# Macaron block on one core: weighings of the attention in pairs, earlier projections at its end, and two weight splits in other places

## The chip, the cores and the metric

The kernel runs on one core of a Trainium2 chip. The metric is the device time of one execution in microseconds (us); lower is better. Engine names as in the profile: PE is TensorE's matmul side and PEld its weight loads, DVE is VectorE, ACT is ScalarE, POOL is GpSimd, SP is SyncE, which here only issues transfers.

## What is computed

One macaron block over 2,048 tokens of width 512: half a mixture of experts, causal attention, half a mixture of experts, each behind a layer norm and added to the residual.

```python
x = x + 0.5 * ffn(layernorm(x))      # 8 experts, the best 2 of each token, width 256, SiLU gate
x = x + attention(layernorm(x))      # 16 query heads, 4 key heads of 32, rotary, causal, softmax, @ wo
x = x + 0.5 * ffn(layernorm(x))      # the same experts once more
```

Everything is float32. The expert matmuls are made of high and low parts of the operands (`WH`, `WL`, `XH`, `XL`): `WH` is a rounded copy of the weights `WR`, `WL` is `WR - WH`, and a product is the sum of three matmuls.

## The kernel before

All engines run fixed programs, tied by semaphores; each engine works through its own queue in order. The stages follow each other: router and layer norm (`*_first`), routing 0 (`dve_route`, `pe_route`, `act_route` with f = 0), 39 expert tiles (`*_experts`), projections of the attention (`*_project`), the attention with the next router inside it (`*_attend`), routing 1 and 39 expert tiles again (f = 1).

**The attention's plan.** `attend_plan` writes one list of steps; each engine walks through it and does its own part of each step. The work is cut into 16 groups G (a block b = G // 4 of 512 queries, one key head, its 4 query heads). Group G has 4b + 4 key tiles k of 128 keys; a tile is numbered n. A tile has four `score` steps (one matmul for each head, line L1674), each followed on ACT by an exponential into a buffer `P4` (L1774). A `weigh` step (L1688) multiplies the four heads' exponentials with V in four narrow matmuls of 32 output columns each, which run side by side in the array, into bank 3; where PE also sums the exponentials, a `sum` of the same form follows (L1706, into bank 4), at a group's last tile also one of `CD` (L1697). Before the change, `weigh` of tile n - 1 stands behind the fourth score of tile n. Groups from 8 on have four `P4` buffers, n modulo 4.

**The tops.** Between the scores stand `top` steps for a later group: a matmul of queries by keys (L998) whose maximum DVE takes (L1011, with a mask L1013). Their banks are 5, 6 and 7 in a ring, and for part of groups 8 to 13 bank 4 as well, lent from one group's `even` to the first `sum` of the next. Scores take banks 0 to 2 in turn (after the last top five banks).

**The sums besides PE.** In groups 8 to 14 POOL adds some tiles into `CH` (`link`, four additions of a head each, L1848), and transfers that accumulate add others, and at last `CH`, into `CD` (`onto`, L1864); POOL issues those. The group's last `weigh` step waits for the last of these transfers. On the diagonal POOL also masks the exponentials (L1834).

**The end of the attention.** After group 15, ACT makes `WH` of four experts (L568, `split1`), the last projections `("proj", 3, c)` run (L1723, four matmuls over the groups 12 to 15, index k, for each c), DVE adds the residual (L1902), takes the statistics and a root by Newton (`norm1`, with a square root on ACT, L341), ACT scales (`scale1`, L1791), PE transposes (`turn`, L389), ACT copies the transposed tile (L400) and the kept residual (`keep`, L1798), and `logits` (L414) and `best` end the router. Banks come from `Ring.take` in the plan's order.

**Routing.** `dve_route` computes the expert tiles' slots and tokens (`TK`, on which the gathers wait), with `EI` (the expert of each tile) behind the large masks `LL`, and `slots` a long matmul of PE (L734). `low_in_between` is one `WL` (L574) inside it, used only for f = 1.

Of the kernel before, what the change touches and what calls it, by code (L numbers as in the profile page):

```python
# [9 lines left out]
NE = 8  # L10
# [581 lines left out]
def dve_route(g, f, R, low_in_between=None):  # L592
# [63 lines left out]
    for h in range(2):  # L656
# [10 lines left out]
        for q in range(2 * h, 2 * h + 2):  # L667
# [1 line left out]
                              ps.HF[:, 1, 8 * q:8 * q + 8].unsqueeze(2).to_broadcast([P, 8, P]),  # L669
                              ALU.is_equal).then_inc(rt.sem, 1)  # L670
            out["LL", q] = rt.up()
    if low_in_between:
        low_in_between()
    dve.tensor_tensor(ps.en, r.ba[:], ps.tl, ALU.add).then_inc(rt.sem, 1)
    dve.wait_ge(rt.sem, rt.up())
    dve.tensor_tensor(r.cj[:], K[:, C_IOTAJ:C_IOTAJ + NJ * NE].rearrange("p (j e) -> p j e", e=NE),
# [5 lines left out]
    dve.wait_ge(rt.sem, rt.up())  # L682
    dve.tensor_copy(r.EI[:], ps.EF).then_inc(rt.sem, 1)
    out["EI"] = rt.up()
    dve.wait_ge(s(f"slots{f}"), 1)
    sl = bk(g, 2)
    if f == 0:
# [834 lines left out]
    return LINKS[n + first_two[1] - k] if k == first_two[0] else LINKS[n]  # L1522


def finish_plan(b):

    todo = [[("proj", b, c)] for c in range(4)]
    todo += [[("stats", b, c)] for c in range(4)]
    todo += [[("store", b), ("solve", b)]]
    todo += [[("scale", b, c)] for c in range(4)]  # L1530
    todo += [[("turn", 4 * b + c)] for c in range(4)]
    return todo + [[("logits", b)], [("best", b)]]


def attend_plan(g):
# [15 lines left out]
    for n, (G, k) in enumerate(TILES):  # L1551
        b = G // 4
        for j in range(4):
# [22 lines left out]
            if j == 3 and n:  # L1576
                if known and known[0][0] <= at and free and n - 1 not in LAST.values():
                    solved.append(known.pop(0)[1])
                    plan.append(("solvemax", solved[0]))
                plan.append(("weigh", n - 1))  # L1580
                if n - 1 in LAST.values():
                    G0 = TILES[n - 1][0]
                    plan.append(("out", G0))
                    free = False
                    put(at + 1, ("recip", G0))
                    put(at + 3, ("even", G0))
                    if G0 % 4 == 3:
                        if b == 1:
                            residual(at + 2, 0)
                        until = at + (34 if b == 1 else 9)  # L1590
                        put(until, ("finish", G0 // 4))
                        residual(until + 62, G0 // 4 + 1)
# [6 lines left out]
            assert told > G, (told, G)  # L1599
    assert not later and not extra and not ahead, (later, extra, len(ahead))  # L1600
    plan += [("weigh", len(TILES) - 1), ("out", 15), ("up1", 4), ("split1", 0), ("split1", 1), ("split1", 2), ("split1", 3), ("recip", 15), ("even", 15)]
    for c in range(4):
        plan += [("proj", 3, c), ("norm1", c), ("scale1", c)] + ([("turn", 12 + c - 2), ("keep", c - 2)] if c >= 2 else [])
    plan += [("turn", 14), ("turn", 15), ("keep", 2), ("keep", 3), ("split1", 4), ("split1", 5), ("split1", 6), ("split1", 7)]
    plan += [("logits", 3), ("best", 3), ("store", 3)]
    ring.set_banks([5, 6, 7], ring.n)
    g.lent, g.back = range(7, 13), {}
# [2 lines left out]
    g.wide = min(4 * step[1] + step[2] for step in plan[last + 8:] if step[0] == "score")  # L1610
    for step in plan:
        if step == ("proj", 3, 0):
            ring.set_banks([5, 6, 7, 0, 2, 1], 5)
        if step == ("score", g.wide // 4, g.wide % 4):
            g.wide_after = {bank: ring.uses[bank] for bank in (5, 6)}
            ring.set_banks([7])
# [36 lines left out]
def pe_attend(g):  # L1653
# [56 lines left out]
    def proj(key):  # L1710
        _, b, c = key
        bank = pe_take(g, key)
        if b == 0 and c == 0:
            pe.wait_ge(s("wo"), 16)
        if b == 3:
            pe.wait_ge(s("exp"), 4 * len(TILES))
        if b == 3 and c < 3:
            pe.wait_ge(s("even"), 15)
            pe.wait_ge(s("norm"), c + 1)
        else:  # L1720
            pe.wait_ge(s("even"), 4 * b + 4)
        for k in range(4):
            ins = pe.matmul(bk(g, bank), a.OTs[b % 2][:, k, c * P:c * P + P], a.WO[:, k, :], start=(k == 0), stop=(k == 3))  # L1723
        ins.then_inc(s(f"full{bank}"), 1)

# [330 lines left out]
def build(nc, d, out):  # L2056
    ctx = ExitStack()
    with ctx:
# [20 lines left out]
        act_first(g)  # L2079
        dve_first(g)  # L2080

        g.routed[0] = dve_route(g, 0, g.R0)
        for e in range(5, NE):
            dve_low(g, 0, e)
        for bank in range(8):
            pe.wait_ge(s(f"free{bank}"), 3)
# [31 lines left out]
        g.routed[1] = dve_route(g, 1, g.R1, low1)  # L2118
        pe_route(g, 1)
        act_route(g, 1)  # L2120
        sp_down1(g)

        def residual_stored():
# [67 lines left out]
```

## Time and profile before

| | |
|---|---|
| median of 3 runs | 1263.03 us (1262.26 to 1265.78) |
| the profiled execution's own time | 1267.54 us |
| its span, first to last instruction | 1266.3 us |
| busy: PE, DVE, ACT, POOL | 1174.0, 905.0, 670.7, 601.7 us |
| mean granted clock of PE | 0.986 of full speed |
| groups 8 to 11 (by the first exponential of each) | 599.67 to 781.32 us |
| groups 12 to 14 | 781.32 to 958.97 us |
| last matmul of group 15, first gather of the second experts | 997.5, 1045.20 us |

All durations below are of the one profiled execution; it took 4.5 us more than the runs' median, so differences are worked out inside it and then taken off the median. A matmul's busy time is modelled with its pipeline in it, so that PE seems full even where it issues late: the intervals between starts tell more than the durations.

### The profile page before, as it was taken

What the parts mean: (1) busy time and instruction counts of PE and PEld (TensorE: products, weight loads), DVE (VectorE), ACT (ScalarE), POOL (GpSimd) and SP (SyncE); (2) the same over time, 40 slices, a digit from 0 to 9 for tenths busy, and PEclk for the clock granted to TensorE, in tenths of its full rate; (3) what the DMA queues carried; (4) which work ended last, traced back from release to release, by engine and by line L of the source; (5) the groups of instructions that cost most, each with busy time, mean ns of one, the idle gap of its engine ahead of it and who ended that gap; (6) DMA issues with size and microseconds to landing.
All of it is one profiled execution on the core that took longest, in us unless ns stands there. A gap on an engine that the chain in (4) does not pass through costs nothing.

```text
span 1266.3 us, 20984 instructions
## 1 busy us (share of the span) xinstructions
PE 1174.0 (93%) x6830; PEld 752.6 (59%) x6837; DVE 905.0 (71%) x2116; ACT 670.7 (53%) x1322; POOL 601.7 (48%) x496
## 2 busy tenths in 40 slices
PE   4899999989999999999999999999999878999996
PEld 3578888858786544444445455445443356777774
DVE  7767777769998676576678787678755775666664
ACT  2545555537666554354456566356577744445442
POOL 5844544313210111001527655556592555888886
PEclk9899999999999999999999999999999989999999
DMA  9923333556530032023345845556632453556565
GB/s 340 366 92 109 108 109 109 175 169 127 94 67 4 35 68 35 1 79 75 83 134 135 168 109 128 176 143 163 148 77 61 144 200 74 100 101 100 103 102 74
DMA packets 68552, 148.44 MB, mean 117 GB/s; under 512 B 8832, under 2 KB 29312, under 8 KB 64448
## 3 DMA queue, kind: packets, MB, share of 16 engines
q0 software_dynamic: 35184, 93.34, 34.3%
q1 hardware_dynamic: 33264, 53.77, 12.4%
q8 instruction: 59, 0.97, 0.3%
q14 instruction: 45, 0.37, 0.1%
HBM read 81.28 MB, written 33.55 MB: 91 GB/s over the span
## 4 chain that ended last, share of the span: by engine, by line
PE 55%; DVE 17%; DMA 10%; issue 7%; POOL 7%; ACT 4%; SPq 0%; DVEq 0%; POOLq 0%; ACTq 0%
PE bank L840 9%; PE bank L1674 8%; PE bank L1688 8%; PE bank L998 7%; PE bank L863 5%; PE bank L1723 4%; DVE PM L1011 4%; POOL out L790 4%; DMA out<-Y,DI 4%; PE bank L1706 4%; DVE bank L1013 3%; PE bank L1433 3%; DMA XG<-xn,TK 2%; DMA CD<-P 2%; PE bank L822 2%
## 5 line engine op out<-in xcount | busy, mean ns | idle before, releaser
L1774 ACT ACTIVATE P<-bank 128x512 f32<-128x512 f32 (+3 forms) x640 | 304.4, 534 | 250.2 <-PE bank L1674 241.1
L1011 DVE TENSOR_REDUCE PM<-bank 128x1 f32<-128x512 f32 x384 | 252.3, 683 | 62.0 <-PE bank L998 61.3
L1674 PE MATMUL bank<-Qs,Ks 98*128 98x512 f32 (+3 forms) x640 | 242.2, 408 | 4.6 <-ACT P L1774 3.4
L998 PE MATMUL bank<-Ks,Qs 96*128 96x512 f32 (+3 forms) x640 | 234.5, 387 | 12.2 <-DVE PM L1013 6.1
L1674 PEld LDWEIGHTS bank<-Qs,Ks 98*128 98x128 f32 x640 | 116.6, 189 | 140.5 <-ACT P L1774 74.2
L1834 POOL TENSOR_SCALAR_AFFINE_SELECT P<-P 128x512 f32<-128x512 f32 x64 | 44.2, 702 | 270.6 <-ACT P L1774 229.1
L998 PEld LDWEIGHTS bank<-Ks,Qs 96*128 96x128 f32 x640 | 121.1, 190 | 60.8 <-DVE PM L1011 22.3
L1688 PE MATMUL bank<-P,V 128*32 128x512 f32 (+3 forms) x1280 | 151.7, 546 | 4.3 <-POOL P L1834 4.3
L1013 DVE CUSTOM_DVE_ANT_0 bank<-bank,KB 128x128 f32<-128x128 f32 (+3 forms) x256 | 124.1, 495 | 40.6 <-PE bank L998 39.9
L790 POOL DMA_INDIRECT out<-Y,DI x78 | 129.1, 1655 | 38.7 <-issue 31.8
L1848 POOL TENSOR_TENSOR CH<-CH,P 128x512 f32<-128x512 f32 x108 | 139.4, 1444 | 14.0 <-ACT P L1774 13.4
L952 DVE TENSOR_TENSOR DL<-W,DH 128x512 fp32r<-128x512 f32 x152 | 98.3, 688 | 41.4 <-ACT DH L913 41.4
L767 POOL DMA_INDIRECT XG<-xn,TK x78 | 93.4, 1198 | 32.6 <-issue 16.5
L913 ACT CAST DH<-W 128x512 fp32r x152 | 86.7, 618 | 20.9 <-issue 20.9
L840 PE MATMUL bank<-WH,XH 128*128 x312 | 92.4, 418 | 0.9 <-issue 0.6
L840 PE MATMUL bank<-WL,XH 128*128 x312 | 85.7, 396 | 1.3 <-DVE XL L934 1.3
L840 PE MATMUL bank<-WH,XL 128*128 x312 | 85.5, 395 | 0.0
L779 POOL DMA_INDIRECT y<-Y,DI x39 | 38.7, 993 | 97.1 <-DVE Y L962 97.1
L934 DVE TENSOR_TENSOR XL<-bank,XH 128x512 fp32r<-128x512 f32 x78 | 53.9, 691 | 35.2 <-ACT XH L893 35.2
L899 ACT ACTIVATE G<-bank 128x256 f32<-128x256 f32 x78 | 29.9, 384 | 84.4 <-PE bank L840 84.4
L893 ACT CAST XH<-bank 128x512 fp32r<-128x512 f32 x78 | 45.8, 587 | 47.2 <-PE bank L822 44.1
L1706 PE MATMUL bank<-P,ones 128*32 128x512 f32 (+3 forms) x664 | 69.0, 487 | 1.3 <-DVE PM L1011 1.3
(194 smaller groups left out, 1935.6 us busy)
## 6 DMA issues: line engine op xcount, KB each, us to landing
CD<-P POOLq DMA_DIRECT2D x17, 1024.0 KB, 6.9
xn<-XN SPq DMA_DIRECT2D x8, 1024.0 KB, 9.5
WR<-L_ffn_w POOLq DMA_DIRECT2D x16, 512.0 KB, 15.2
XO<-y POOLq DMA_DIRECT2D x8, 1024.0 KB, 9.5
WR<-L_ffn_w SPq DMA_DIRECT2D x16, 512.0 KB, 7.9
CD<-P SPq DMA_DIRECT2D x7, 1024.0 KB, 4.7
CD<-CH POOLq DMA_DIRECT2D x7, 1024.0 KB, 6.9
XA<-y POOLq DMA_DIRECT2D x24, 256.0 KB, 4.0
```

What stands on the lines that cost most here:

```text
L767: pool.indirect_dma_start(out=x.XG[:, j % NG, :], out_offset=None, in_=g.xnd[f][:, :], in_offset=bass.IndirectOffsetOnAxis(ap=r.TK[:, j:j ...
L790: pool.indirect_dma_start(out=g.out.rearrange("t (h d) -> (t h) d", h=2), out_offset=bass.IndirectOffsetOnAxis(ap=r.DI2[:, h, j:j + 1], ax ...
L840: ins = pe.matmul(bk(g, 2 + j % 2), part[:, k * P:k * P + P], w[:, bass.ds(ev[j] * 2048 + k * 512, 512)], start=(n == 0 and k == 0), stop= ...
L952: ins = dve.tensor_tensor(x.DL[:, k, :], W.W3[:, bass.ds(e * 1024 + k * 512, 512)], DHf[:, k, :], ALU.subtract)
L998: pe.matmul(bk(g, bank)[:, 0:n], g.Qs[b][0:96, G % 4 * 4 + h, c * P:c * P + P], g.Ks[0:96, G % 4, k * BQ:k * BQ + n], start=True, stop=Tru ...
L1011: dve.tensor_reduce(dst, bk(g, bank)[:, 0:n], AX.X, ALU.max).then_inc(s(f"free{bank}"), 1)
L1013: dve.tensor_tensor_reduce(out=bk(g, bank)[:, 0:n], in0=bk(g, bank)[:, 0:n], in1=g.KB[:, CB_MASK + BQ - n:CB_MASK + BQ], scale=1.0, scalar ...
L1674: pe.matmul(bk(g, bank)[:, o:BQ], g.Ks[0:98, G % 4, k * P:k * P + P], g.Qs[G // 4][0:98, G % 4 * 4 + j, o:BQ], start=True, stop=True).then ...
L1688: ins = pe.matmul(bk(g, 3)[32 * h:32 * h + 32, o:BQ], g.V[:, k, q * HD:q * HD + HD], a.P4[buffer_of(n)][:, h, o:BQ], start=(k == 0), stop= ...
L1706: ins = pe.matmul(bk(g, 4)[32 * h:32 * h + 32, o:BQ], g.ones[:], a.P4[buffer_of(n)][:, h, o:BQ], start=fresh, stop=last)
L1774: act.activation(a.P4[buffer_of(n)][:, j, o:BQ], bk(g, score_bank(g, i))[:, o:BQ], ACT.Exp, scale=scale).then_inc(s("exp"), 1)
L1848: ins = pool.tensor_tensor(to[:, h, :], two[:, h, :], one[:, h, :], ALU.add)
```

## The change

Four edits:

1. `weighed_at`: in groups 8 to 14 the weighings of tiles k - 1 and k (k odd) stand one behind the other after the fourth score of the tile after k. In the other groups nothing changes.
2. The last projections: the first three matmuls of each c wait only for groups 12 to 14, the fourth for group 15's part. The ring gets bank 4 as a seventh one. Steps after the third c are reordered: turn 13 and keep 1 before the last tile is scaled.
3. The last `split1` (ACT's `WH` of the eighth expert) moves behind ACT's exponential of routing 1.
4. `low_in_between` moves from before `EI` to after it, and is now used in routing 0 as well: one of the three `WL` that DVE made after routing 0 stands before the wait for `slots`.

```diff
@@ dve_route
-    if low_in_between:
-        low_in_between()
     dve.tensor_tensor(ps.en, r.ba[:], ps.tl, ALU.add).then_inc(rt.sem, 1)
...
     out["EI"] = rt.up()
+    if low_in_between:
+        low_in_between()
     dve.wait_ge(s(f"slots{f}"), 1)
@@
+def weighed_at(n):
+    if not n:
+        return ()
+    G, k = TILES[n - 1]
+    if G < 8 or G == 15:
+        return (n - 1,)
+    return (n - 2, n - 1) if k % 2 else ()
@@ attend_plan
-                plan.append(("weigh", n - 1))
+                plan += [("weigh", m) for m in weighed_at(n)]
...
-    for c in range(4):
-        plan += [("proj", 3, c), ("norm1", c), ("scale1", c)] + ([("turn", 12 + c - 2), ("keep", c - 2)] if c >= 2 else [])
-    plan += [("turn", 14), ("turn", 15), ("keep", 2), ("keep", 3), ("split1", 4), ("split1", 5), ("split1", 6), ("split1", 7)]
+    for c in range(3):
+        plan += [("proj", 3, c), ("norm1", c), ("scale1", c)]
+    plan += [("turn", 12), ("keep", 0), ("proj", 3, 3), ("turn", 13), ("norm1", 3), ("keep", 1), ("turn", 14), ("scale1", 3)]
+    plan += [("turn", 15), ("keep", 2), ("keep", 3), ("split1", 4), ("split1", 5), ("split1", 6)]
...
-            ring.set_banks([5, 6, 7, 0, 2, 1], 5)
+            ring.set_banks([5, 6, 7, 0, 2, 1, 4], 6)
@@ pe_attend, proj
-        if b == 3 and c < 3:
             pe.wait_ge(s("even"), 15)
-            pe.wait_ge(s("norm"), c + 1)
...
         for k in range(4):
+            if b == 3 and k == 3:
+                if c < 3:
+                    pe.wait_ge(s("norm"), c + 1)
+                else:
+                    pe.wait_ge(s("even"), 16)
@@ build
-        g.routed[0] = dve_route(g, 0, g.R0)
-        for e in range(5, NE):
+        g.routed[0] = dve_route(g, 0, g.R0, low0)
+        for e in range(6, NE):
...
         act_route(g, 1)
+        act_high(g, 1, NE - 1)
```

**Place 1: PE at the start of group 10.** The first piece is PE's program before: scores (L1674 or L1685), tops (L998) and a weighing (L1688 or L1699) of one `P4` buffer. Names such as bank1 are pairs of banks.

```order
L998 MATMUL bank3<-Ks_137,Qs2_135 128x512
L1688 MATMUL bank1<-P40_155,V_138 32x512 x4
L1674 MATMUL bank1<-Qs2_135,Ks_137 128x512
L998 MATMUL bank3<-Ks_137,Qs2_135 128x512
L1674 MATMUL bank0<-Qs2_135,Ks_137 128x512
L998 MATMUL bank2<-Ks_137,Qs2_135 128x512
```

The same place in the changed program:

```order
L1685 MATMUL bank1<-Qs2_135,Ks_137 128x512
L998 MATMUL bank2<-Ks_137,Qs2_135 128x128
L998 MATMUL bank3<-Ks_137,Qs2_135 128x512
L1699 MATMUL bank1<-P40_155,V_138 32x512 x4
L1699 MATMUL bank1<-P41_156,V_138 32x512 x4
L1685 MATMUL bank0<-Qs2_135,Ks_137 128x512
```

The weighing of buffer 0 moved four scores back, behind those of the following tile, and stands directly before that of buffer 1; two returns from narrow to wide matmuls became one.

**Place 2: PE at the end of the attention.** Before, with the semaphores that a row waits for (L1723 is the projection, one group of four for each c):

```order
L1723 MATMUL bank<-WO,OT_160 128x512 [waits even,norm,exp,free5]
L1723 MATMUL bank<-WO,OT_160 128x512 x3
L1723 MATMUL bank<-WO,OT_160 128x512 [waits even,norm,exp,free6]
L1723 MATMUL bank<-WO,OT_160 128x512 x3
L1723 MATMUL bank<-WO,OT_160 128x512 [waits even,norm,exp,free7]
L1723 MATMUL bank<-WO,OT_160 128x512 x3
```

After (L1737 is the same line):

```order
L1737 MATMUL bank<-WO,OT_160 128x512 [waits even,exp,free5]
L1737 MATMUL bank<-WO,OT_160 128x512 x2
L1737 MATMUL bank<-WO,OT_160 128x512 [waits norm]
L1737 MATMUL bank<-WO,OT_160 128x512 [waits even,exp,free6]
L1737 MATMUL bank<-WO,OT_160 128x512 x2
L1737 MATMUL bank<-WO,OT_160 128x512 [waits norm]
```

The wait for group 15's normalized part moved from the first matmul of each c to its fourth.

**Place 3: DVE in routing 0.** Before, from `EI` on:

```order
L683 CAST EI_89<-bank 128x39
L688 SCALAR_TENSOR_TENSOR TD_90<-bank,KF_72 128x39
L690 CAST TI_91<-bank 128x39
L692 TENSOR_SCALAR TK_92<-TI_91 128x39
L699 COPY DW_94<-bank 128x39
L701 TENSOR_TENSOR DI_93<-TD_90,bank 128x39
L574 TENSOR_TENSOR WL_70<-WR_69,WH_68 128x2048 x3
L934 TENSOR_TENSOR XL_115<-bank,XH_114 128x512
```

After:

```order
L681 CAST EI_89<-bank 128x39
L574 TENSOR_TENSOR WL_70<-WR_69,WH_68 128x2048
L688 SCALAR_TENSOR_TENSOR TD_90<-bank,KF_72 128x39
L690 CAST TI_91<-bank 128x39
L692 TENSOR_SCALAR TK_92<-TI_91 128x39
L699 COPY DW_94<-bank 128x39
L701 TENSOR_TENSOR DI_93<-TD_90,bank 128x39
L574 TENSOR_TENSOR WL_70<-WR_69,WH_68 128x2048 x2
```

One `WL` moved in front of `TD`, whose first operand comes from PE's slots.

## Rows read from the trace of the kernel before

**Rows 1.** The page: the chain that ended last by engine, the exponentials, the tops.
```profile
PE 55%; DVE 17%; DMA 10%; issue 7%; POOL 7%; ACT 4%; SPq 0%; DVEq 0%; POOLq 0%; ACTq 0%
...
L1774 ACT ACTIVATE P<-bank 128x512 f32<-128x512 f32 (+3 forms) x640 | 304.4, 534 | 250.2 <-PE bank L1674 241.1
L1011 DVE TENSOR_REDUCE PM<-bank 128x1 f32<-128x512 f32 x384 | 252.3, 683 | 62.0 <-PE bank L998 61.3
```

**Rows 2.** Windows, groups 10 and 11: length, busy PE, PEld, DVE, ACT, POOL, clock, DMA, GB/s.
```profile
701.80:742.10 40.30, 39.31 (x241) 20.21 (x241) 32.02 (x75) 24.19 (x50) 26.28 (x24) 1.00 0.79 161
742.10:781.32 39.22, 38.79 (x240) 20.46 (x240) 31.89 (x72) 24.32 (x52) 24.99 (x23) 1.00 0.45 105
```

**Rows 3.** Timeline, a weighing among tops and scores: start, us, engine, line, operation.
```profile
920.88 0.39 PE L1674 MATMUL bank<-Qs,Ks 98*128 98x512 f32 x1
921.11 0.40 PE L998 MATMUL bank<-Ks,Qs 96*128 96x512 f32 x1
921.44 1.06 PE L1688 MATMUL bank<-P,V 128*32 128x512 f32 x8
922.43 0.50 PE L1674 MATMUL bank<-Qs,Ks 98*128 98x512 f32 x1
922.77 0.34 PE L998 MATMUL bank<-Ks,Qs 96*128 96x384 f32 x1
```

**Rows 4.** Timeline of PE, a weighing with a sum directly behind it.
```profile
954.12 1.06 PE L1688 MATMUL bank<-P,V 128*32 128x512 f32 x8 [1.38 <-POOL P L1834]
954.98 1.07 PE L1706 MATMUL bank<-P,ones 128*32 128x512 f32 x8
```

**Rows 5.** Waits from 600 to 960 us: who waited for whom, us, times, longest.
```profile
PEld bank L998 <- DVE PM L1011: 12.4, 34, 1.2
```

**Rows 6.** Timeline of POOL in groups 13 and 14.
```profile
873.21 2.51 POOL L1848 TENSOR_TENSOR CH<-CH,P 128x512 f32<-128x512 f32 x2 [0.20 <-ACT P L1774]
...
926.71 10.07 POOL L1848 TENSOR_TENSOR CH<-CH,P 128x512 f32<-128x512 f32 x8 [0.53 <-ACT P L1774]
```

**Rows 7.** The chain that ended last, end of group 14: start, us, what.
```profile
955.03 6.88 DMA CD<-CH
```

**Rows 8.** Timeline, last projections to logits; in brackets the idle time and its releaser.
```profile
1000.32 10.54 PE L1723 MATMUL bank<-WO,OT 128*128 128x512 f32 x24 [2.36 <-DVE OT L1954]
...
1006.03 0.20 ACT L341 ACTIVATE sm<-sm 128x1 f32<-128x1 f32 x1
...
1014.77 0.70 DVE L1902 TENSOR_TENSOR bank<-bank,XO 128x512 f32<-128x512 f32 x1 [0.60 <-PE bank L1723]
...
1018.07 0.78 ACT L1791 ACTIVATE XN<-bank,sm 128x512 f32<-128x512 f32 x1 [1.23 <-DVE sm L1991]
...
1019.95 0.63 PE L389 MATMUL bank<-K,XN 128*128 128x128 f32 x4 [0.86 <-ACT XO L1798]
...
1021.74 1.54 PE L414 MATMUL bank<-xT,RT 128*32 128x128 f32 x32 [1.16 <-ACT XO L1798]
...
1023.32 0.29 DVE L423 COPY xT<-bank 128x128 f32<-128x128 f32 x1 [5.29 <-PE bank L414]
```

**Rows 9.** Timeline, routing 1.
```profile
1022.05 7.32 ACT L568 CAST WH<-WR 128x2048 fp32r<-128x2048 f32 x4
...
1030.93 0.18 DVE L649 TENSOR_SCALAR bank<-wd 128x16 f32<-128x16 f32 x1 [0.34 <-ACT wd L715]
```

**Rows 10.** Timeline, routing 0 and the first expert tile.
```profile
57.54 0.20 DVE L683 CAST EI<-bank 128x39 int32<-128x39 f32 x1
58.94 0.20 DVE L688 SCALAR_TENSOR_TENSOR TD<-bank,KF 128x39 f32<-128x39 f32 x1 [1.20 <-PE bank L734]
...
59.71 6.75 DVE L574 TENSOR_TENSOR WL<-WR,WH 128x2048 fp32r<-128x2048 f32 x3
...
64.80 1.19 PE L840 MATMUL bank<-WH,XH 128*128 x4
...
67.31 1.17 PE L840 MATMUL bank<-WL,XH 128*128 x4 [1.31 <-DVE XL L934]
```

More of the change, by code:

```diff
@@ L2080, in build, with low0 @@
         dve_first(g)
-        g.routed[0] = dve_route(g, 0, g.R0)
-        for e in range(5, NE):
+        def low0():
+            dve_low(g, 0, 5)
+        g.routed[0] = dve_route(g, 0, g.R0, low0)
+        for e in range(6, NE):
             dve_low(g, 0, e)
```

## The prediction

> **What bounds the kernel now.** I read the page first: PE holds 55% of the chain that ended last, DVE 17%, transfers 10%, POOL 7% [rows 1]. PE is the engine to shorten, but not everywhere, so I went to the windows of single groups, then to the timeline of PE alone, where intervals between starts are real while durations are modelled. In groups 10 and 11 DVE is busy 32.02 of 40.30 and 31.89 of 39.22 us (79% and 81%), ACT about 60% [rows 2]. PE sets the pace there, with DVE not far behind.
>
> The timeline shows what a weighing costs beside its own work. A score starts 0.23 us before the top behind it (920.88 to 921.11). A top directly ahead of a weighing takes 0.33 (921.11 to 921.44), 0.10 more. The weighing takes 0.99 until the score behind it starts (921.44 to 922.43), and that score 0.34 until the next top (922.43 to 922.77), 0.11 more than 0.23 [rows 3]. A weighing with a block of the same narrow form behind it takes only 0.86 (954.12 to 954.98) [rows 4], 0.13 less than 0.99. So each trip from wide to narrow matmuls and back costs 0.10 + 0.13 + 0.11 = 0.34 us. I use 0.33.
>
> In groups 13 and 14 something else sets the pace for a while. POOL's additions into CH run with gaps of only 0.20 and 0.53 us ahead of them, at 2.51 us for two and 10.07 for eight, so about 1.26 each, four a link [rows 6]. Group 14 ends on the last accumulating transfer, 955.03 + 6.88 = 961.91 [rows 7]. PE's gains between the first exponentials of tile 4 and that end can't shorten the group.
>
> **The change, part by part.** *Pairs.* Groups 8 to 11 have 12 tiles each and 12 to 14 have 16: 24 + 24 = 48 pairs, so 48 trips fewer. As PE time that is 48 x 0.33 = 15.8 us. No instruction is added or removed.
>
> Groups 8 to 12 hold 32 pairs, 10.6 us of PE. How much comes through? A pair of weighings keeps PE away from scores and tops for 0.86 + 0.99 = 1.85 us. ACT can have three scores in hand, 3 x 0.534 = 1.6 us, DVE three or, with the lent bank 4, four tops, 3 x 0.683 = 2.0 or 2.7 us [rows 1]. So DVE hardly runs dry and ACT, with 40% to spare [rows 2], may idle 0.2 us at no cost. But DVE's share rises: two tiles that took about 6.5 us take 0.33 less, so 81% becomes 85%. PE's loads of tops already waited for DVE 34 times, 12.4 us, over the stretch [rows 5]; more of that will come. Below, nothing of the 10.6 arrives (DVE takes all); above, all of it. The rows are nearer to the upper end, since DVE idles 7 to 8 us in each of groups 10 and 11 and a group needs to give back only 6 x 0.33 = 2 us. I take three quarters: 7.9 us.
>
> Groups 13 and 14: three things remain. The pair across each group's start and the pair of tiles 0 and 1 lie ahead of POOL's run, 2 x 0.33. And the order helps: the weighing of tile 2 now stands behind the scores of tile 4, so the exponentials that POOL's run begins with come one weighing, about 1 us, earlier relative to the rest. POOL waited for ACT there [rows 6], though only 0.5 us in group 14 directly, with a DMA issue and an earlier link between. I take 1.7 us for group 13, whose last two pairs count again (it isn't POOL that ends it), and 1.3 for group 14: 3.0 us, from 0.7 to 4.5. The other pairs are hidden by POOL and the transfers and cost nothing. What is queued behind the moved weighings: the exponential of tile n + 2 needs the buffer of n - 2, which is weighed directly after the scores of n; four scores of n + 1 lie between, so no new wait. The masks of the diagonal have more time than before. Attention: 7.9 + 3.0 = 10.9 us.
>
> *A rule beside it.* The trace gives 0.33 us a trip. The Trainium skill (TensorEngine Tiling (Array Packing), Key Properties) says that changing the tiling mode drains TensorE, and (TensorE: Matmul & The Clock Gate, Part 2: What happens when you issue a matmul) that the wavefront needs some 128 cycles to leave, which matmuls of one mode hide behind each other. By that alone, two drains at the full clock of these windows (1.00 granted, 2.4 GHz [rows 2]) are an estimated 0.11 us a trip, and 48 trips 5 us. The rows show three times that, and the sum goes by the rows.
>
> *The end of the attention.* PE waited 2.36 us for the first part of group 15's output before it began the last projections [rows 8]. Now three of the first four matmuls run in that time. What is late next: the first root on ACT, at 1006.03, behind the four expert casts and a table load. That doesn't move, and DVE waits for it. From there on DVE's chain of each c paces, so PE's 2.36 us come down to what DVE waited for PE, 0.60 us at the fourth add [rows 8] and some 0.1 before. Against that, turn 13's copy (about 0.5 us) now stands ahead of the last root and delays it 0.2: the last scaled tile is ready about 0.5 us earlier, 18.07 + 0.78 - 0.5 = 18.35 (less 1000). Before, the last turn started at 1019.95, behind a `keep` that freed its bank, and the logits at 1021.74, again behind a `keep` [rows 8]. With bank 4 in the ring and the copies of turns 13 and 14 done early, the turn starts at 18.4 and takes 0.63, and the logits follow at 19.05 for 1.54, with the copy of 0.6 inside: 20.6. DVE's copy moves from 1023.32 to about 1020.55: **2.8 us**. Bounds: 1.5, if one `keep` still gates, and 3.3, if the last root isn't delayed.
>
> *The eighth cast.* Four casts take 7.32 us, 1.83 each, ahead of the exponential of routing 1, for which DVE waited 0.34 us [rows 9]. With three, ACT is ahead by 1.8 us: 0.34 us gained. The cast itself ends long before the `WL` that needs it.
>
> *WL in routing 1.* It stood and stands ahead of `slots`' reader in the same DVE run: the same sum, 0.
>
> *WL in routing 0.* DVE was free at 57.74 and got the slots at 58.94. A `WL` takes 6.75 / 3 = 2.25, so until 59.99: `TD`, the tokens, the gather and the first expert matmuls are 1.05 us later, 64.80 becomes 65.85. But there the low matmuls waited 1.31 us for DVE's `XL`, behind three `WL`: 67.31 [rows 10]. Now two are left, DVE is free before the tile is, and the low matmuls start directly behind the four high ones: 65.85 + 1.19 = 67.05. Gain 0.25 us; at worst, if `XL` stays the last, 1.05 lost.
>
> *Carried to the end.* The second experts follow, tile after tile; a start 3.1 us earlier shifts them whole, since nothing they load is late: the gathers wait for the tokens.
>
> **Sum.** 10.9 + 2.8 + 0.34 + 0.25 = 14.3 us. In the profiled execution's time 1267.54 - 14.3 = 1253.2; its distance to the runs' median is 4.5, and 1263.03 - 14.3 = 1248.7. I say 1249.
>
> **The rivals.**
> 1. *DVE takes much of it back.* The tops, now in bursts of eight or nine between longer pauses, meet DVE's other work (sums, roots, residual adds), the ring runs full and PE stalls as it does at rows 5, or ACT does with three banks in the eight scores in a row. For: 81% busy. Against: the fourth bank. The attention then yields 2.5 to 6 instead of 10.9: 1254 to 1257.5, middle 1256. The Trainium skill (TensorEngine Tiling, PSUM Bottleneck) warns of just this: column tiling speeds up TensorE, not the emptying of PSUM. Chance 0.22.
> 2. *The pairs do nothing.* The return cost isn't saved, because a weighing of other weights behind a weighing pays it too (rows 4 show a sum behind a weighing, with equal moving data), or POOL and transfers bound more groups than I think. Left: 3.4 us, 1259.6, not told from no change. Chance 0.08.
> 3. *Slower.* The pause of 1.85 us outlasts what DVE has in hand wherever the ring holds three banks and one isn't filled yet: two tops, 1.4 us, so 0.5 us of DVE lost in each pair. If DVE bounds those groups, 48 pairs lose 24 - 15.8 = 8 us net, less the other 3.4: 1268. It decides only where DVE has under 8% idle; rows 2 show 19 to 21%. Chance 0.04.
> 4. *More.* Waits behind masks and for banks shrink too, all 10.6 us arrive and group 13's and 14's upper values: 1244.5. Chance 0.06.
>
> **How the numbers follow.** The forecast, 1245.5 to 1253 by its own bounds, has 0.60. A measurement can tell about 0.3%, 3.8 us: faster is below 1259.2. Faster: 0.60 + 0.22 + 0.06 = 0.88; same 0.08; slower 0.04. The range takes the forecast and rival 1 but for its edge: 1244.5 to 1257.
>
> **What the changed profile would show.** Two weighings in a row with 0.86 to 0.88 us between their starts, if the saving is real; with 0.99, rival 2. Groups 10 and 11 each near 38.5 us or below, DVE's share at 83 to 86%; if they stay above 39.5 with more waits of L998 for L1011, rival 1. POOL's additions in group 14 at 1.26 us each with no more gaps than now, and group 14's last transfer still the last thing before its sum. The first projection at the last sum of group 15, without 2.36 us; the fourth add without its wait; the logits directly behind the last turn. The first low matmuls of the experts at 67.05, without a wait for `XL`. I'm wrong above all if the share of three quarters is, and if the second experts don't carry the shift.

## The result, and the profile after

The changed kernel took 1284.36 us in the median of 4 runs (1281.59 to 1288.41), beside 1264.40 us (1262.26 to 1272.29, 4 runs) of the kernel before. The ratio is 1.0139, 95% interval [1.0109, 1.0170]: slower by 1.4% (by the two medians alone 20.0 us, 1.6%), where 1249 us and faster were forecast. Its profiled execution took 1283.19 us, with a span of 1281.9 us and a mean granted clock of 0.976.

Below, "groups 8 to 14" is the time from the first exponential of group 8 to the first of group 15, read from the windows of each kernel; a single group's length is likewise from its first exponential to the next group's. It was 359.45 us before and is 380.36 us now, 20.9 more. The stretch behind it is 2.7 us shorter. It began at 601.11 us before and at 598.54 now; over the profiles of all kernels here that start lies between 597.2 and 601.1, so the 2.6 us ahead of it show no effect of the change.

First what was forecast and came. The timeline of PE, two weighings in a row, at the full clock:

```profile
960.71 1.92 PE L1699 MATMUL bank<-P,V 128*32 128x512 f32 x16
962.57 0.73 PE L1685 MATMUL bank<-Qs,Ks 98*128 98x512 f32 x2
```

From the start of the pair to the next score are 1.86 us, as forecast (1.85): here the trip saves what it should. Now group 10, the worst. The windows of groups 10 and 11, with the columns of [rows 2]:

```profile
704.22:750.68 46.46, 40.60 (x241) 21.82 (x241) 36.01 (x75) 23.98 (x51) 26.26 (x24) 0.89 0.68 136
750.68:793.88 43.20, 39.82 (x240) 21.58 (x240) 32.53 (x72) 24.08 (x52) 25.42 (x23) 0.96 0.46 105
```

They took 40.30 and 39.22 us before [rows 2]. (Both pairs of windows begin 0.6 to 1.7 us ahead of the group's first exponential; counted from it, group 10 went from 40.39 to 46.51 us and group 11 from 39.17 to 43.15.) DVE is busy 4 us longer in group 10 with the same 75 instructions, and the clock is no longer 1.00. One instruction of DVE explains the first, and the long wait of PE in which the clock fell. The timeline of DVE, then POOL, then PE in group 10:

```profile
712.92 5.15 DVE L1964 TENSOR_TENSOR OT<-OT,SM 128x512 f32<-128x512 f32 x1
717.99 1.27 DVE L1011 TENSOR_REDUCE PM<-bank 128x1 f32<-128x512 f32 x2
...
712.50 1.29 POOL L1895 DMA_DIRECT2D XO<-y  x1 [7.08 <-DMA XO<-y]
713.30 4.21 POOL L1862 TENSOR_TENSOR CH<-P,P 128x512 f32<-128x512 f32 x3
720.65 1.27 POOL L1862 TENSOR_TENSOR CH<-P,P 128x512 f32<-128x512 f32 x1 [3.15 <-ACT P L1788]
...
711.52 0.40 PE L1685 MATMUL bank<-Qs,Ks 98*128 98x512 f32 x1
712.58 0.50 PE L998 MATMUL bank<-Ks,Qs 96*128 96x512 f32 x1 [0.65 <-DVE PM L1011]
...
718.72 0.80 PE L998 MATMUL bank<-Ks,Qs 96*128 96x512 f32 x1 [4.89 <-DVE PM L1011]
...
720.71 3.64 PE L1699 MATMUL bank<-P,V 128*32 128x512 f32 x16
```

The product `OT<-OT,SM` is the step `even`: it scales the last group's output by the reciprocal sums. It took 5.15 us. The same product before, in the same group, in DVE's and POOL's timelines of the kernel before:

```profile
710.63 0.69 DVE L1950 TENSOR_TENSOR OT<-OT,SM 128x512 f32<-128x512 f32 x1
...
711.77 3.03 POOL L1848 TENSOR_TENSOR CH<-P,P 128x512 f32<-128x512 f32 x2
```

There it ended at 711.32, before POOL's first additions into `CH` began. Now both ran together. DVE could empty no top, the ring was full, PE waited 4.89 us, and the pair of weighings behind it took 3.64 us instead of 1.92, at half the clock. Windows before, during and behind that:

```profile
708.00:714.40 6.40, 5.18 (x39) 2.80 (x27) 4.97 (x10) 4.40 (x8) 1.90 (x2) 1.00 0.99 274
714.60:724.60 10.00, 5.88 (x21) 2.04 (x22) 7.28 (x10) 0.60 (x1) 4.17 (x4) 0.50 0.70 106
724.80:735.00 10.20, 10.10 (x54) 6.43 (x53) 9.19 (x23) 7.82 (x16) 7.47 (x7) 1.00 0.51 105
```

The granted clock was 0.50 (1.2 of 2.4 GHz) for ten microseconds. They begin 0.7 us into PE's wait (its last matmul ahead of it ended at 713.84) and last until 6 us behind it. The product took 1.25, 1.25, 1.70 and 1.46 us behind groups 7, 8, 10 and 11, each with POOL's first additions beside it, but 0.67 and 0.68 behind groups 12 and 13. In groups 8 to 14 the clock is at half for 34.1 us in all, 6.8 before.

PE's loads of tops waited longer for DVE. Waits between 600 and 980 us (columns as in [rows 5], 12.4 us and 34 times before, up to 960):

```profile
PEld bank L998 <- DVE PM L1011: 33.6, 63, 5.3
```

The end of group 14, PE's timeline, with ACT's wait that led to it:

```profile
970.40 2.75 ACT L1788 ACTIVATE P<-bank 128x384 f32<-128x384 f32 x8 [3.27 <-DMA CD<-P]
...
970.95 1.35 PE L1685 MATMUL bank<-Qs,Ks 98*128 98x256 f32 x3 [1.99 <-ACT P L1788]
972.22 1.94 PE L1699 MATMUL bank<-P,V 128*32 128x512 f32 x8
973.93 1.94 PE L1717 MATMUL bank<-P,ones 128*32 128x512 f32 x8
...
980.59 1.04 PE L1708 MATMUL bank<-CD,ones 128*32 128x512 f32 x8
```

The weighings and sums of tiles 12 and 13 run at half clock (1.94 us each), and group 14's last step is now bound by PE, no longer by the transfer of [rows 7].

### The profile page after: what moved, and what is told of

Read it like the earlier page. It is cut to its first block, busy times and chain, and to the rows that moved or that the text cites. A ratio compares the mean times of both kernels' runs of the same rounds, so it can differ in the third digit from the quotient of the medians.

```text
span 1281.9 us, 20981 instructions
## 1 busy us (share of the span) xinstructions
PE 1175.8 (92%) x6830; PEld 761.0 (59%) x6837; DVE 910.3 (71%) x2116; ACT 668.5 (52%) x1322; POOL 599.6 (47%) x496
## 4 chain that ended last, share of the span: by engine, by line
PE 56%; DVE 23%; issue 7%; DMA 6%; POOL 4%; ACT 3%; SPq 0%; DVEq 0%; ACTq 0%; POOLq 0%
PE bank L840 11%; PE bank L1699 9%; PE bank L1685 7%; PE bank L998 7%; PE bank L863 5%; DVE PM L1011 5%; POOL out L790 4%; DVE bank L1013 4%; PE bank L1717 4%; PE bank L1737 3%; DMA XG<-xn,TK 3%; PE bank L1433 3%; DMA out<-Y,DI 2%; PE bank L822 2%; DVE CD L1928 2%
## 5 line engine op out<-in xcount | busy, mean ns | idle before, releaser
L998 PE MATMUL bank<-Ks,Qs 96*128 96x512 f32 (+3 forms) x640 | 242.3, 397 | 25.9 <-DVE PM L1011 16.6
L1685 PE MATMUL bank<-Qs,Ks 98*128 98x512 f32 (+3 forms) x640 | 240.0, 405 | 7.7 <-ACT P L1788 7.4
L1685 PEld LDWEIGHTS bank<-Qs,Ks 98*128 98x128 f32 x640 | 118.3, 191 | 109.0 <-issue 65.3
L998 PEld LDWEIGHTS bank<-Ks,Qs 96*128 96x128 f32 x640 | 122.0, 191 | 87.4 <-DVE PM L1011 43.8
L1699 PE MATMUL bank<-P,V 128*32 128x512 f32 (+3 forms) x1280 | 151.5, 566 | 1.4 <-POOL P L1848 1.4
L767 POOL DMA_INDIRECT XG<-xn,TK x78 | 92.5, 1186 | 32.2 <-issue 18.6
```

Source lines behind the costliest of these rows:

```text
L767: pool.indirect_dma_start(out=x.XG[:, j % NG, :], out_offset=None, in_=g.xnd[f][:, :], in_offset=bass.IndirectOffsetOnAxis(ap=r.TK[:, j:j ...
L998: pe.matmul(bk(g, bank)[:, 0:n], g.Qs[b][0:96, G % 4 * 4 + h, c * P:c * P + P], g.Ks[0:96, G % 4, k * BQ:k * BQ + n], start=True, stop=Tru ...
L1685: pe.matmul(bk(g, bank)[:, o:BQ], g.Ks[0:98, G % 4, k * P:k * P + P], g.Qs[G // 4][0:98, G % 4 * 4 + j, o:BQ], start=True, stop=True).then ...
L1699: ins = pe.matmul(bk(g, 3)[32 * h:32 * h + 32, o:BQ], g.V[:, k, q * HD:q * HD + HD], a.P4[buffer_of(n)][:, h, o:BQ], start=(k == 0), stop= ...
```

## The experiments

Each kernel below is the changed one with the edit shown, but for the first, which starts from the kernel before. The figure of "groups 8 to 14" is from each one's own profile, a single execution. Those of e3 and e6 lie off their medians (1279.48 us against 1274.12, 1277.79 against 1281.85); the others lie within 3.2 us of theirs.

**Both halves apart.** One kernel takes `weighed_at` alone into the kernel before; the other keeps the rest and weighs singly.

```diff
 e1_pairs_only (kernel before)
-                plan.append(("weigh", n - 1))
+                plan += [("weigh", m) for m in weighed_at(n)]
 e2_rest_only (changed kernel)
     G, k = TILES[n - 1]
-    if G < 8 or G == 15:
-        return (n - 1,)
-    return (n - 2, n - 1) if k % 2 else ()
+    return (n - 1,)
```

> The kernel before with the pairs of weighings alone, nothing of the other three edits. The changed kernel's attention is 22 us longer over groups 8 to 14 and its end about 3 us shorter. Both theories of the loss (A: POOL's first addition of a group now falls onto DVE's product OT x SM and stops it; B: bursts of scores and tops with longer pauses run the rings full) put the loss in the pairs: 1282 to 1290 us. If the loss came from the other edits, it stays near 1264.

> The changed kernel with single weighings everywhere, so the end of the attention, the moved cast and the moved WL alone. Both theories: the 3.1 us of the end and some 0.3 to 1.4 us at routing 0, so 1258 to 1261 us with the kernel before at 1263 to 1264. Near 1264 if the end's gain is lost behind it.

Pairs alone: 1286.97 us, ratio 1.0189 [1.0138, 1.0240], groups 8 to 14 in 377.79 us. The rest alone: 1263.34 us, 0.9970 [0.9946, 0.9993], 358.41 us. So the pairs carry the whole loss and the other edits gain about 3 us.

**The collision taken away.** POOL's first addition of a group waits for `even`.

```diff
 e3_pool_waits_even, pool_attend, first link of a group
             pool.wait_ge(s("onto"), 16 * (ONTO[MERGED[G - 1]] + 1))
+        if new:
+            pool.wait_ge(s("even"), G)
```

> The changed kernel, and POOL's first addition of each group waits until DVE's product OT x SM of the group before is done. Theory A (DVE's product is stopped by POOL's additions, PE's tops wait for it, and the clock falls after the stall): the product is back at 0.7 us in groups 8 to 12, the 5.0 us stall in group 10 and its 10.2 us at half clock are gone, 1264 to 1274 us. Theory B (bursts fill the rings): no change, 1281 to 1287 us, or a little more for the added wait.

1274.12 us, 1.0068 [1.0046, 1.0090], 372.93 us: no `even` is long any more (0.68 to 0.69 us), and some 10 of the 20 us are back by the medians, not all. The clock was expected to recover with it, but is at half for 27.3 us here; in group 10 for 3.4 instead of 10.2. What remains at each group's start is seen in PE's timeline of group 10 of this kernel:

```profile
711.98 0.50 PE L998 MATMUL bank<-Ks,Qs 96*128 96x512 f32 x1 [0.67 <-DVE PM L1011]
...
713.66 0.50 PE L998 MATMUL bank<-Ks,Qs 96*128 96x512 f32 x1 [0.41 <-DVE PM L1011]
...
714.93 0.80 PE L998 MATMUL bank<-Ks,Qs 96*128 96x512 f32 x1 [0.34 <-DVE PM L1013]
```

DVE is behind there, with the reciprocal, two transposes and `even` between its tops. The weighing of tile 0 used to stand just here; now PE waits 1.42 us in three pieces and does the weighing afterwards.

**Which pairs.** One kernel without the pair of tiles 0 and 1 of each group (41 pairs), one with only those seven.

```diff
 e4_pairs_from_tile2
-    if G < 8 or G == 15:
+    if G < 8 or G == 15 or k < 2:
 e6_pairs_01_only
+    if G < 8 or G == 15 or k >= 2:
```

> The changed kernel, but the weighings of tiles 0 and 1 of each group stand singly as before; pairs begin with tiles 2 and 3, 41 pairs of 48. Then POOL's first addition (it needs tile 2's exponentials) stands against DVE's product as in the kernel before. Theory A: no collision, and the saved trips come through in part, 1252 to 1266 us. Theory B: 41 of 48 pairs still bunch the work, 1278 to 1284 us.

> The changed kernel with only the pair of tiles 0 and 1 of groups 8 to 14, 7 pairs, the complement of the run that pairs from tile 2 on. Theory A (POOL's first addition stops DVE's product, PE's tops wait, the clock falls): this alone brings most of the loss, DVE's product takes 1.2 to 5 us in groups 8 to 12, 1272 to 1282 us. Theory B or C alone: 7 of 48 pairs, within 3 us of the variant with single weighings, 1260 to 1266 us.

Without: 1265.79 us, 1.0006 [0.9990, 1.0022], 360.97 us. Only those seven: 1281.85 us, 1.0125 [1.0103, 1.0146], 373.22 us. Taking them away gives 18.6 us, adding them to single weighings costs 18.5 (1281.85 against 1263.34, two chips): seven of 48 pairs are nearly the whole loss. Not all of it is the collision: in group 10 of e6 `even` took 0.69 us, ended ahead of POOL's additions, and the group still took 44.11 us, against 40.41 in e2, with 6.8 us of it at half clock.

**The collision made without any pair.** All weighings single; `even` stands two places later in the plan, so that it meets POOL's first additions.

```diff
 e8_even_later_no_pairs (with weighed_at of e2_rest_only)
-            put(at + 3, ("even", G0))
+            put(at + (5 if G0 >= 7 else 3), ("even", G0))
```

> Single weighings everywhere, but DVE's product OT x SM of groups 7 to 14 stands two scores later in the plan, where POOL's first additions run. No pair is in this kernel. Theory A: the product takes over 1.2 us in several groups and PE's tops wait for it, 1266 to 1280 us. Without a collision of the two engines it stays near the single variant, 1262 to 1265 us.

1272.28 us, 1.0045 [1.0027, 1.0062], 369.59 us. All seven `even` took 1.67 to 1.77 us. From DVE's and POOL's timelines:

```profile
711.52 2.97 POOL L1860 TENSOR_TENSOR CH<-P,P 128x512 f32<-128x512 f32 x2 [0.71 <-ACT P L1786]
711.61 0.14 DVE L1013 DVE_READ_ACCUMULATOR2_ANT PM<- 128x1 f32 x1
711.61 1.75 DVE L1962 TENSOR_TENSOR OT<-OT,SM 128x512 f32<-128x512 f32 x1
```

Against e2, the same kernel with `even` in its place, this costs 9 us (1272.28 - 1263.34, measured apart) with no pair at all. So moving `even` into POOL's additions costs much by itself. Two things besides the longer product are in these 9 us: the step `even` also lends bank 4 to the tops, so they get it two scores later, and group 9, which is 4.3 us longer, ran 6.8 us at half clock, in e2 none. Their shares weren't measured apart.

e3 is 8.3 us above e4 (1274.12 - 1265.79). Most of that I put down to lost cover at the groups' starts, but it isn't shown: e3 also makes POOL wait, and is at half clock for 27.3 us, e4 for 10.2. That 8.3 and 9 make 17, near the 18.6, is no proof of the division.

**The other pairs, in two parts.** Pairs of tiles before the diagonal in groups 8 to 13 (22), and pairs on the diagonal in groups 8 to 14 (14).

```diff
 e5_pairs_off_diagonal
+    if G < 8 or G >= 14 or k < 2 or k >= 4 * (G // 4):
 e7_pairs_diagonal_only
+    if G < 8 or G == 15 or k < 4 * (G // 4):
```

> The changed kernel with pairs only in groups 8 to 13, only from tile 2 on and only before the diagonal: 22 pairs, no collision at the group's start. Theory C (a weighing is the one work that PE can do while it waits for another engine, and a pair leaves the stretch before it without one; that costs about 1 us at each long wait, and these stand on the diagonal and in group 14) and A: 22 x 0.34 = 7.5 us of trips, most of it comes, so 3 to 7 us below the variant with single weighings (1263.3): 1256 to 1260 us. Theory B (bursts between longer pauses lose everywhere): 1262 to 1268 us.

> The changed kernel with pairs only on the diagonal of groups 8 to 14, 14 pairs, trips worth 14 x 0.34 = 4.8 us. Theory C: the long waits there (table loads behind the square root, the last transfer of group 14) lose their filler, some 1 us each, and group 14 about 2, so the gain is eaten: 1261 to 1266 us, and PE's wait after the root is 2.5 us instead of 1.5. If pairs were harmless there: 1258.5 to 1260.

1263.93 us, 0.9980 [0.9966, 0.9993], 360.52 us; and 1263.47 us, 0.9982 [0.9964, 1.0000], 359.72 us. Neither is better than single weighings (358.41), and e5 missed the 1256 to 1260 us expected of it. PE's timelines show where a part of the saving goes: single weighings (e2) first, then e5, then e7.

```profile
768.07 0.60 PE L1060 MATMUL bank<-K,M 128*8 128x128 f32 x4 [0.33 <-DVE M L1051]
```

```profile
769.68 0.60 PE L1060 MATMUL bank<-K,M 128*8 128x128 f32 x4 [1.25 <-DVE M L1051]
...
839.22 0.55 PE L1685 MATMUL bank<-Qs,Ks 98*128 98x512 f32 x1 [2.45 <-ACT P L1788]
```

```profile
652.75 0.66 PE L1685 MATMUL bank<-Qs,Ks 98*128 98x512 f32 x1 [2.37 <-ACT P L1788]
```

The second and third are scores that wait while ACT takes a root, with a table load of 1.28 us before and one behind it; in the kernel before they waited 1.26 us (group 12) and 1.33 (group 8). They grew by 1.0 to 1.2 us, and the wait for `M` (the found maxima) by 0.9, a weighing's length; a weighing that stood there had moved. One such wait takes back about three trips. The rest of what e5 and e7 lost isn't at these waits: group 9 was 2.3 and 1.3 us longer than in e2, and group 14 of e7 3.4, each with 3.4 to 6.8 us at half clock where e2 had none.

**Fillers left in place.** Four kernels measured together, beside 35 runs of the kernel before: the diagonal pairs without group 14; group 14's two diagonal pairs alone; e5 without two pairs, those that had filled the waits above; and all pairs from tile 2 on in groups 8 to 13 without three such.

```diff
 e9_diagonal_8_to_13
+    if G < 8 or G >= 14 or k < 4 * (G // 4):
 e10_pairs_14_diagonal
+    if G != 14 or k < 12:
 e11_off_diagonal_fillers
+    if G < 8 or G >= 14 or k < 2 or k >= 4 * (G // 4) or (G, k // 2) in ((11, 3), (12, 5)):
 e12_pairs_8_to_13_fillers
+    if G < 8 or G >= 14 or k < 2 or (G, k // 2) in ((8, 5), (11, 3), (12, 5)):
```

> The changed kernel with pairs only on the diagonal (the last four tiles) of groups 8 to 13: 12 pairs, 4.1 us of PE time. If group 14's two pairs caused its 3.4 us at half clock (theory: the late weighings of tiles 12 and 13 pile up behind the last transfer), group 14 takes 49.5 us as without pairs, no stretch at half clock in it, and the time is about 1260 against 1263.5 with them (ratio to the kernel before about 0.9955). If the half clock there came by chance of place, group 14 stays at 52.9 and the time at 1263.5.

> The changed kernel with the pairs (12, 13) and (14, 15) of group 14 alone, all else weighed singly. If these two make the stall and the fall of the clock by themselves, group 14 takes 52.9 us instead of 49.5 with 6.8 us at half clock, and the time is 1265.5 to 1266.5, 3 us above that of single weighings. If it needs the pairs before it, group 14 stays at 49.5 and the time at 1263.

> Pairs in groups 8 to 13 from tile 2 to the diagonal, as in the run with 22 pairs, but tiles 6 and 7 of group 11 and 10 and 11 of group 12 singly: 20 pairs. Theory of the lost filler: PE's wait for the found maxima in group 11 falls from 1.47 to about 0.4 us, that behind the root in group 12 from 2.61 to 1.44, and the time by some 2 us less 0.7 for the two trips, to about 1262.3. If the waits are the same however the weighings stand, nothing changes or 0.7 us are lost: 1264 to 1264.6.

> Pairs in groups 8 to 13 from tile 2 on, also on the diagonal, but three pairs singly where a weighing filled a wait of PE (10 and 11 of group 8, 6 and 7 of group 11, 10 and 11 of group 12): 31 pairs, 10.5 us of PE time by the trip's price. If the trip's price arrives where no wait takes the filler, this is the fastest: 1257 to 1260, ratio 0.993 to 0.996. If the ring of banks or DVE gives back what PE saves, it stays at 1262 to 1263.5 as with single weighings.

| | us (median) | ratio to before | groups 8 to 14 |
|---|---|---|---|
| before | 1265.80 | | 359.45 |
| e9 | 1262.78 | 0.9970 [0.9946, 0.9995] | 359.53 |
| e10 | 1262.69 | 0.9973 [0.9945, 1.0001] | 357.73 |
| e11 | 1262.13 | 0.9968 [0.9944, 0.9993] | 357.30 |
| e12 | 1259.40 | 0.9950 [0.9921, 0.9979] | 356.78 |

*Fillers.* In e11 the two waits are back, in PE's timeline:

```profile
766.24 0.60 PE L1060 MATMUL bank<-K,M 128*8 128x128 f32 x4 [0.33 <-DVE M L1051]
...
834.90 0.50 PE L1685 MATMUL bank<-Qs,Ks 98*128 98x512 f32 x1 [1.27 <-ACT P L1788]
```

With two pairs fewer than e5 it is 3.2 us shorter in the groups. Of that, groups 11 and 12, where the two pairs stood, give 0.9 and 0.7 us. That is as the lost filler would have it, and against waits that don't depend on the order. Another 1.7 are group 9's, whose plan is the same in both: 3.4 us of it were at half clock in e5, none in e11. The medians of the two, measured apart, can't be told from each other.

*Group 14: my expectation fell.* With its pairs alone (e10) the group took 49.2 us at a full clock, and without any pair in it (e9) 51.6 us with 3.4 us at half clock. PE's timeline of e10 and the window behind its wait, then the same two of e9:

```profile
950.48 0.77 PE L1685 MATMUL bank<-Qs,Ks 98*128 98x256 f32 x2 [2.15 <-ACT P L1788]
```

```profile
950.50:953.80 3.30, 3.30 (x27) 1.34 (x31) 0.00 (x0) 2.18 (x7) 2.07 (x3) 1.00 0.69 141
```

```profile
949.19 1.32 PE L1699 MATMUL bank<-P,V 128*32 128x512 f32 x8 [2.52 <-POOL P L1848]
```

```profile
950.00:953.20 3.20, 3.20 (x16) 1.20 (x8) 0.00 (x0) 1.69 (x6) 1.49 (x2) 0.50 0.60 123
```

What differs, as I read it, is how early PE and ACT arrive. ACT's exponential waits for a `CD<-P` transfer there, 3.1 us before and in e5 and e11, 4.3 us in e7, e9 and e12, where the diagonal of group 13 has pairs. (The changed kernel, e1, e3 and e4 have these pairs too, and pairs from the start of group 14 on as well; there it was 3.3.) POOL's additions and the transfers come no earlier, so PE's saving becomes a longer wait. In e7, e9 and e12 the clock fell behind waits of PE of 2.5 to 3.4 us. But the length of this wait alone doesn't decide: the changed kernel and e1 have the same plan there and the same wait, 1.99 us, and the clock fell in one and not in the other. What decides stays open.

*The best version.* e12 is faster than both kernels, by 0.5% against the one before. Single weighings with the same other edits (e2) have 0.3% of that, and the intervals of the two overlap, so a gain of the pairs themselves isn't told from none. Its 31 pairs are 10.5 us of PE by the trip's price, and groups 8 to 14 gained 1.6 against single weighings. Windows of groups 10 and 11, e2 first, then e12:

```profile
700.02:740.43 40.41, 39.42 (x241) 20.29 (x240) 31.91 (x74) 24.27 (x50) 26.31 (x24) 1.00 0.77 158
740.43:779.60 39.17, 38.73 (x240) 20.40 (x239) 31.97 (x70) 24.31 (x50) 25.02 (x23) 1.00 0.47 109
```

```profile
699.27:738.23 38.96, 38.12 (x241) 21.08 (x240) 31.47 (x76) 23.89 (x50) 26.25 (x25) 1.00 0.79 163
738.23:777.24 39.01, 38.30 (x240) 20.99 (x239) 31.57 (x70) 24.14 (x51) 25.03 (x24) 1.00 0.48 113
```

In group 10 five pairs gave 1.45 us, 85% of five trips. In group 11 four gave 0.16 of 1.4. So the share that comes through depends on the group. PE's waits before tops (L998) over 598 to 958 us rose from 3.5 to 6.0 us, and the loads' waits for DVE, 12.4 us in 34 pieces before [rows 5], were 18.8 in 52, so some 2.5 us are given back to DVE. Two groups work against the rest, both with 3.4 us at half clock that e2 hasn't: group 9 is 1.35 us longer, and group 14, which has no pair, 2.2. The other five gained 5.1 us, group 12 with 3.4 us fewer at half clock.

**What the clock costs.** No experiment held the clock fixed, but the profiles have the same group under the same plan at either level. Group 9 before and in e2, then group 14 in the changed kernel and in e1 (columns of [rows 2]):

```profile
656.25:703.44 47.19, 44.70 (x289) 23.67 (x290) 35.88 (x95) 26.52 (x56) 27.25 (x25) 0.96 0.55 135
```

```profile
654.39:700.02 45.63, 43.23 (x289) 23.22 (x290) 35.82 (x95) 26.57 (x55) 27.27 (x25) 1.00 0.58 140
```

```profile
925.68:978.90 53.22, 48.74 (x281) 22.75 (x280) 23.19 (x52) 31.88 (x66) 35.66 (x32) 0.94 0.44 100
```

```profile
925.75:976.25 50.50, 46.04 (x281) 22.02 (x280) 23.19 (x52) 31.90 (x67) 35.69 (x32) 1.00 0.45 103
```

That is 1.56 us for 3.4 at half clock and 2.72 for 6.8, so 0.40 to 0.46 for each. Over groups 8 to 14, in us:

| | length | of it at half clock |
|---|---|---|
| e2, e10, e11 | 358.41, 357.73, 357.30 | 3.4 each |
| before, e5, e12 | 359.45, 360.52, 356.78 | 6.8 each |
| e4, e7, e9 | 360.97, 359.72, 359.53 | 10.2 each |
| e8 | 369.59 | 10.2 |
| e6 | 373.22 | 20.5 |
| e3, e1 | 372.93, 377.79 | 27.3 each |
| changed | 380.36 | 34.1 |

The changed kernel has 30.7 us more at half clock than e2. In 4.2 of them PE stood still in group 10, where the clock costs nothing. The other 26.5 are, as an estimate from these two prices, 11 to 12 of the 22 us between the two. So about half of the loss is the stalls' own, and half is the slower clock that came with them. What makes the clock fall isn't worked out, but it did so mostly in kernels with the pair of tiles 0 and 1.

## Why the prediction was wrong, point by point

- **The trip's price, 0.33 to 0.34 us: right.** A pair takes 1.86 us at the full clock, and group 10 of e12 gave 0.29 us a pair.
- **"Groups 13 and 14 ... the order helps": the step that failed.** I saw that the weighing moves back and that the exponentials of tile 2 come about 1 us earlier, and booked it as a gain for POOL in these two groups. For groups 8 to 12 the order had no term, and I never asked what DVE did at that moment. In each of groups 8 to 14 POOL's first additions begin with those exponentials. In the kernel before they began between 0.21 us ahead of the end of `even` (group 9) and 1.37 us behind it (group 14), 0.45 in group 10. Moved earlier, they met its product of two SBUF operands in groups 8 to 12: 0.69 us became 1.25 to 5.15. In groups 13 and 14 it stayed at 0.67 and 0.68. Making such a collision costs 9 us (e8), with a later lent bank and more half clock in them, and removing it gives back 10 (e3).
- **"What is queued behind the moved weighings ... no new wait": the second failure.** I checked who waits *for* the weighings, not what PE does where they stood. There they covered waits: for DVE at each group's start, for the root's table loads, for the found maxima. Each of the three uncovered waits followed in e5 and e7 grew by about 1 us, three trips' worth. At the groups' starts the lost cover is argued from the timelines, and from group 10 of e6, 3.7 us longer without a collision; what it costs there by itself isn't measured (e3 against e4, 8.3 us, has more in it).
- **The share of three quarters: wrong.** With the pair of tiles 0 and 1 it was negative. Without collisions (e12) it was 85% in group 10 and some 11% in group 11.
- **Groups 13 and 14, "PE's gains can't shorten the group": right, and incomplete.** PE's gains there lengthen a wait instead, and behind it the clock fell (2.1 to 3.4 us in groups 14 of e9, e12 and e7, against 49.5).
- **The clock** stood in no term. The changed kernel ran 34.1 us of groups 8 to 14 at half, e2 3.4. By the two prices above that is an estimated half of the loss.
- **The end of the attention: right.** Forecast 2.8 us. From the last sum of group 15 to DVE's copy of the logits it was 1023.32 - 997.53 = 25.79 us, and is 23.08 now (1016.39 to 1039.47), 2.7 less. The first projection starts 0.36 us behind that sum, without the 2.36 us of [rows 8], and the last turn starts at 1037.04, 0.05 us behind its scaled tile. The rows of the changed kernel:

```profile
1016.39 0.43 PE L1717 MATMUL bank<-P,ones 128*32 128x128 f32 x8
1016.75 10.57 PE L1737 MATMUL bank<-WO,OT 128*128 128x512 f32 x24
...
1037.04 0.66 PE L389 MATMUL bank<-K,XN 128*128 128x128 f32 x4 [0.52 <-ACT XN L1805]
1037.63 1.81 PE L414 MATMUL bank<-xT,RT 128*32 128x128 f32 x32
...
1039.47 0.29 DVE L423 COPY xT<-bank 128x128 f32<-128x128 f32 x1 [3.29 <-PE bank L414]
```

- **WL in routing 0: right in kind, larger in size.** The `WL` took 3.16 us, not 2.25. It began while POOL was still making two `WL` of its own, until 57.90 (48.81 + 9.09), and ended 2.16 us behind that; so it looks like the same meeting of DVE and POOL, which the forecast had at nothing here too. No run tests it. The tokens came as late as forecast (1.04 us, 59.98 against 58.94) only because `EI` was earlier by 0.76. But the first low matmuls start at 66.58 with no wait for `XL`, 0.73 us earlier than in [rows 10] (0.25 forecast):

```profile
48.81 9.09 POOL L574 TENSOR_TENSOR WL<-WR,WH 128x2048 fp32r<-128x2048 f32 x2
...
56.90 3.16 DVE L574 TENSOR_TENSOR WL<-WR,WH 128x2048 fp32r<-128x2048 f32 x1
59.98 0.18 DVE L688 SCALAR_TENSOR_TENSOR TD<-bank,KF 128x39 f32<-128x39 f32 x1
...
65.55 1.19 PE L840 MATMUL bank<-WH,XH 128*128 x4
66.58 1.09 PE L840 MATMUL bank<-WL,XH 128*128 x4
```

- **The eighth cast: right.** DVE's wait of 0.34 us for `wd` [rows 9] is gone in the changed kernel.
- **All the other edits together:** forecast 3.4 us, and e2 took 3.3 us less than the runs of before beside it (1266.65).
- **The rivals.** "Slower" was given 0.04, for DVE running dry behind a pair. It was the other way round: DVE was late, not idle, and PE waited for it. "DVE takes much back" describes what is left without the pairs of tiles 0 and 1. It put the time at 1254 to 1257.5, where these kernels took 1259.4 (e12) to 1265.8 (e4). Neither names `even`. The range, 1244.5 to 1257, took in "DVE takes much back" but for its edge and left "slower" out.

## What to carry to other kernels

When an instruction moves back on its engine, list what it covered where it stood: the waits right beside it in the timeline. Where it filled a wait wholly, the move costs about the instruction's whole length there (0.9 to 1.2 us at the three places followed), however much each trip saves. And when something comes earlier, look at what each other engine does at that microsecond; here a DVE product stood within 0.5 us of POOL's additions in five groups, and 9 us hung on it. Leave single what fills a wait, and the loss is gone: e12 is 0.5% faster than the kernel before, though most of that may be the other edits'. And compare the clock before the lengths: two profiles of one plan differed by 2.7 us in a group by it.

## What the runs showed of the hardware

- **A DVE product with both operands in SBUF beside POOL's additions.** It takes 0.69 us with POOL elsewhere. Where it began inside one of POOL's additions it took 1.25 to 1.77 us and ended 0.55 to 0.56 us behind that addition, and POOL's next addition lasted 1.71 to 1.73 us instead of 1.27. In group 10 it took 5.15 us (5.14 in e1) and ended 0.56 us behind three additions in a row, though it began 0.38 us ahead of the first. The Trainium skill (GPSIMD Engine Reference, 8. Key points) says that POOL shares its SBUF interfaces with VectorE and contends with instructions that have two SBUF inputs; the Trainium skill (SBUF — State Buffer, SBUF: two separate sides) calls it an exclusive lock for a whole instruction, the other one blocked. The 1.25 to 1.77 us agree; the 5.15 us go past one instruction. Which of the two starts first mattered too: in group 13 of the changed kernel the product began 0.43 us ahead of POOL's addition and took 0.67 us. Why it got no turn in group 10 no run here shows. What sets these two cases apart is that POOL's issue of the transfer `XO<-y` (712.50, 1.29 us) was still on record when the product began, with the additions directly behind it. The issue alone doesn't do it: in e3, where the additions wait, the product began 0.56 us into it and took 0.69. Additions directly behind that issue last 1.76 to 1.79 us in group 10 of the kernel before as well, with no product beside them, so their length isn't the product's doing.
- **The clock beside a stall.** The granted clock fell to 0.50 (1.2 GHz) for 10 us within a wait of PE of 4.89 us (group 10), and at the end of group 14 behind waits of 1.99 and 2.52 us. Behind 2.15 us (e10) and behind 1.99 us in e1 it stayed at 1.00. In e6 it fell for 6.8 us in group 14 (928.46 to 935.29) behind waits of only 0.75 and 0.68 us. So no single wait tells it, and the rows don't tell what else decides. At half clock a group of the same plan was longer by 0.40 to 0.46 us for each such microsecond.
